# Graph layers on one core: weighted neighbour rows in fixed places with TensorE's source pass as a loop, and edge feature dots as GpSimd products summed by VectorE

## The reference, cut to what matters

```python
# layer 0: attention over the edges that end in a node
h = x @ Wn.T + bn
e = edge_attr @ We.T + be
a = leaky_relu(sum((h[src] + e) * attn, -1), 0.01)
a = softmax of a over the edges with the same dst
x = layernorm(x + relu(segment_sum(h[src] * a, dst)))
# layer 1: mean over neighbours (the roles turn: grouped by src, neighbour is dst)
mean = segment_sum(x[dst], src) / max(count(src), 1)
x = layernorm(x + x @ W1.T + b1 + mean @ W2.T + b2)
```

## Time and profile before

| | |
|---|---|
| median of the runs | 1409.51 us |
| the profiled execution's own time | 1417.53 us |
| its span, first to last instruction | 1415.7 us |
| TensorE busy | 1199.2 us, 85% of the span |
| VectorE busy | 1014.9 us, 72% |
| ScalarE busy | 705.8 us, 50% |
| GpSimd busy | 750.6 us, 53% |
| mean granted TensorE clock | 0.924 |

### The profile page before, as it was taken

How to read it: one execution, slowest core, us unless ns; L and a number is a source line. 1 busy time by engine, 2 the same in 40 slices (tenths; PEclk the granted TensorE clock), 3 DMA queues, 4 the chain that set the end, 5 groups by cost and what they waited for, 6 DMA issues and landing times.

```text
span 1415.7 us, 24884 instructions
## 1 busy us (share of the span) xinstructions
PE 1199.2 (85%) x6829; PEld 1043.3 (74%) x6829; DVE 1014.9 (72%) x3558; ACT 705.8 (50%) x1643; POOL 750.6 (53%) x731
## 2 busy tenths in 40 slices
PE   5988968990099999949999999999988888888884
PEld 5977847880078888838888888888877777777773
DVE  8377897888455555349999999999986656565551
ACT  4655564550034444427777766667763343434332
POOL 1047772767767777744444106656532555556533
PEclk9989999995589999979999999999998888988887
DMA  7779885979436666557777778999962332223211
GB/s 232 256 156 218 198 251 160 280 214 362 148 65 93 101 95 93 71 132 247 244 238 243 250 242 297 311 329 323 326 226 60 90 89 92 86 92 92 90 50 40
DMA packets 118168, 254.24 MB, mean 180 GB/s; under 512 B 23705, under 2 KB 63272, under 8 KB 118084
## 3 DMA queue, kind: packets, MB, share of 16 engines
q1 hardware_dynamic: 75738, 187.26, 41.6%
q0 software_dynamic: 40128, 64.45, 20.1%
q10 hardware_dynamic: 2218, 1.53, 0.3%
HBM read 175.67 MB, written 130.44 MB: 216 GB/s over the span
## 4 chain that ended last, share of the span: by engine, by line
PE 71%; DVE 9%; issue 8%; DMA 5%; ACT 4%; POOL 2%; SPq 1%; ACTq 0%; DVEq 0%; POOLq 0%
PE bank L1378 41%; PE bank L1367 8%; PE bank L1355 5%; PE bank L1427 3%; PE bank L1431 3%; PE bank L1521 3%; PE bank L1277 3%; DVE stats L957 3%; DVE X L784 2%; DMA X<-in_x,idx_src 2%; ACT aggn L631 2%; ACT sel L685 1%; PE bank L1314 1%; DVE xin L784 1%; POOL X L482 1%
## 5 line engine op out<-in xcount | busy, mean ns | idle before, releaser
L1378 PE MATMUL bank<-w1T,xT 128*128 128x256 f32 x1968 | 481.3, 392 | 1.8 <-ACT yout L594 1.8
L1378 PEld LDWEIGHTS bank<-w1T,xT 128*128 128x128 f32 x1968 | 379.1, 197 | 55.9 <-ACT xT L584 2.2
L492 POOL DMA_INDIRECT order_scratch<-pay,rank_i x200 | 195.8, 979 | 218.4 <-DVE xin L784 90.3
L589 ACT ACTIVATE std<-stats,eps_c 128x4 f32<-128x4 f32 x271 | 80.5, 298 | 278.0 <-DVE stats L957 278.0
L584 ACT ACTIVATE xT<-bank 128x512 f32<-128x512 f32 x296 | 176.8, 598 | 82.7 <-PE bank L1367 78.1
L594 ACT ACTIVATE yout<-bank,rstd 128x256 f32<-128x256 f32 x492 | 203.9, 480 | 0.7 <-DVE rstd L1023 0.5
L532 POOL DMA_INDIRECT z_scratch<-xin,idx_out x100 | 156.3, 1563 | 53.9 <-ACT xin L711 30.7
L957 DVE BATCH_NORM_STATS2 stats<-bank 128x6 f32<-128x512 f32 x246 | 167.8, 691 | 10.3 <-PE bank L1378 10.2
L957 DVE BATCH_NORM_STATS2 stats<-xin 128x6 f32<-128x512 f32 x240 | 154.6, 685 | 22.1 <-DMA xin<-z_scratch 22.1
L1378 PE MATMUL bank<-w2T,xT 128*128 128x256 f32 x400 | 126.8, 447 | 50.5 <-issue 49.8
L1355 PE MATMUL bank<-sel,agg 128*128 128x196 f32 x800 | 156.2, 339 | 0.0
(11 more groups left out here) (248 smaller groups left out, 1729.3 us busy)
## 6 DMA issues: line engine op xcount, KB each, us to landing
z_scratch<-in_x SPq DMA_DIRECT2D x125, 400.0 KB
xin<-z_scratch SPq DMA_DIRECT2D x97, 512.0 KB
out_rows<-yout SPq DMA_DIRECT2D x97, 512.0 KB, 3.2
kB<-sorted_scratch SPq DMA_DIRECT2D x50, 256.0 KB, 3.5
yout<-low_digits_scratch SPq DMA_DIRECT2D x50, 128.0 KB, 6.6
yout<-keys_scratch SPq DMA_DIRECT2D x50, 128.0 KB, 5.7
yout<-in_edge_attr SPq DMA_DIRECT2D x12, 512.0 KB, 5.8
order_scratch<-pay,rank_i POOLq DMA_INDIRECT x200
```

What stands on the lines that cost most here:

```text
L492: g.indirect_dma_start(out=order_dram[k], out_offset=bass.IndirectOffsetOnAxis(ap=rank_i[k][:, t:t + 1], axis=0), in_=pay[:, t, :], in_off ...
L1378: ins = mm(to, buf[:, jj, c, 0:n], w[:, c, :], start=not bias and i == 0 and c == 0, stop=i == len(terms) - 1 and c == 1)
```

## The change

It has two parts that do not touch each other.

**Edge feature dots.** `u` is made as 128 equal rows (`u_b`) by a product with 128 columns where there was one. GpSimd multiplies each loaded chunk by it in place (14 `tensor_tensor`, twelve of 128x1024 and two of 128x128), and VectorE sums each row of 128 into `pay` (14 `tensor_reduce`). Seven of the sums stand among the one-hots, after every second group from the 13th on; seven come behind the bias work. TensorE loses 98 turns and 196 small products, ScalarE 25 copies, and VectorE 25 high one-hots, which go to ScalarE (two a group where there was one; on the source side it stays one). SyncE reloads a buffer when its sum is done.

**Source pass.** ScalarE multiplies the four neighbour tiles of a turn by their factors and writes them to tiles 0 to 3 or 4 to 7 of X. The four `sel` tiles become one comparison without a factor. TensorE now reads fixed places, so its turns 4 to 23 become a loop, four turns a round.

```diff
+BY_ACT = (2, 1)
-            for c in range(4, NEC + FT + 1 - NEC * EC):
-                sp.wait_ge(s_eaT, 2 * (c - 3))
+            for c in range(4, NCH):
+                sp.wait_ge(s_eau, c - 3)
                 load_edges(c)
                 copy_x(2)
-            sp.wait_ge(s_eaT, Q)
+            sp.wait_ge(s_eau, NCH)
...
-            pool.wait_ge(s_eau, 1)
+            pool.wait_ge(s_wcp, 4)
+            for c in range(NCH):
+                pool.wait_ge(s_ea[c % 4], 16 * (c // 4 + 1))
+                part = chunk_rows(c)
+                n, k = part.shape[0], part.shape[1]
+                g.tensor_tensor(part, part, u_b[0:n, :].unsqueeze(1).to_broadcast([n, k, DE]), ALU.mult).then_inc(s_eap, 1)
+
+            pool.wait_ge(s_eau, NCH)
...
             def high_onehots(k, q):
-                n = k * Q + q
-                wait(act, s_hotA, n - 3)
-                t = GT * q + GT - 1
-                o = gap_hi[n % 4]
-                made = gap(o, iota16[:, 0:HC], -1.0, dig_f[k][:, 1, t:t + 1])
-                is_zero(onehot_hi[:, t, :], o, made).then_inc(s_hotA, 1)
+                for i in range(BY_ACT[k]):
+                    t = GT * q + GT - BY_ACT[k] + i
+                    n = hots_before(k, q) + i
+                    wait(act, s_hotA, n - 3)
+                    o = gap_hi[n % 4]
+                    made = gap(o, iota16[:, 0:HC], -1.0, dig_f[k][:, 1, t:t + 1])
+                    is_zero(onehot_hi[:, t, :], o, made).then_inc(s_hotA, 1)
...
+            def weigh_neighbours(q, u):
+                act.wait_ge(s_nw, q + 1)
+                wait(act, s_agg[SRC], 2 * (q - 1))
+                for j in range(GT):
+                    rows = X[:, bass.ds(q * GT + j, 1), 0:D].rearrange("p a c -> p (a c)")
+                    a.activation(X[:, u % 2 * GT + j, 0:D], rows, ACT.Copy,
+                                 scale=rstd[:, 4 + u % 2, j:j + 1]).then_inc(s_stage, 1)
+
+            weigh_neighbours(0, 0)
...
+                if in_range(q, 0, Q - 1):
+                    weigh_neighbours(q + 1, u + 1)
                 if in_range(q, 0, Q - 2):
                     root_neighbours(q + 2, u)
...
+            def edge_dots(c):
+                t = chunk_tile(c)
+                part = chunk_rows(c)
+                n, k = part.shape[0], part.shape[1]
+                if c == NCH - 1:
+                    then(v.memset(pay[:, FT:T, 2], 0.0))
+                dve.wait_ge(s_eap, c + 1)
+                v.tensor_reduce(pay[0:n, t:t + k, 2], part, X_AXIS, ALU.add).then_inc(s_eau, 1)
...
-                    if t % GT < GT - 1:
+                    if t % GT < GT - BY_ACT[k]:
                         ts(onehot_hi[:, t, :], iota16[:, 0:HC], dig_f[k][:, 1, t:t + 1], None, ALU.is_equal)
                     if t % GT == GT - 1:
                         ins.then_inc(s_onehot, 1)
+                        if k == DST and t % (2 * GT) == GT - 1 and t >= 12 * GT:
+                            edge_dots((t - 12 * GT) // (2 * GT))
...
-                dve.wait_ge(s_rc[slot], 2 * turn + 2)
-                for j in range(GT):
-                    ins = ts(sel[par][:, j, :], kB[par][:, j, :], keyc[SRC][:, bass.ds(q * GT + j, 1)],
-                             rstd[:, slot, j:j + 1], ALU.is_equal, ALU.mult)
-                ins.then_inc(s_sel[SRC], 1)
+                v.tensor_tensor(sel[par][:], kB[par][:], keyc[SRC][:, now].unsqueeze(2).to_broadcast([P, GT, P]),
+                                ALU.is_equal).then_inc(s_sel[SRC], 1)
...
-            edge_dots()
+            for c in range((Q - 12 + 1) // 2, NCH):
+                edge_dots(c)
             starts(DST)
...
+                        pe.wait_ge(s_stage, GT * q + 2 * p + 2)
                         for jj in range(2):
                             for c in range(2):
-                                rows = X[:, bass.ds(q * GT + 2 * p + jj, 1), c * P:(c + 1) * P].rearrange("p a c -> p (a c)")
+                                rows = X[:, u % 2 * GT + 2 * p + jj, c * P:(c + 1) * P]
...
-            for q in range(Q + 1):
-                by_src(q, q // 4, q % 4)
+            steps(pe, Q + 1, 4, 4, 2, by_src)
```

More of the change, by code:

```diff
@@ L73, in build @@
     NEC = FT // EC
+    NCH = NEC + FT + 1 - NEC * EC
     NCOPY, CR = 125, 5
@@ L301, in build @@
         s_carry = sem("carry_added")
+        s_nw = sem("neighbour_weights")
+        s_stage = sem("neighbours_weighted")
         def wait_apart(eng, sem, value):
@@ L316, in grp, with chunk_tile, chunk_rows @@
                 .rearrange("p a f -> p (a f)")
+        def chunk_tile(c):
+            return c * EC if c < NEC else NEC * EC + c - NEC
+        def chunk_rows(c):
+            t = chunk_tile(c)
+            return edge_rows[c % 4][0:P if t < FT else LT, 0:EC if c < NEC else 1, :]
         def spread(dram, q):
@@ L622, in _ @@
             a.copy(v_b[:], bank[3][:, 0:D])
-            a.copy(u_c[:], bank[4][:, 0:1])
+            a.copy(u_b[:], bank[4][:, 0:DE])
             a.copy(c0[:], bank[5][:, 0:1]).then_inc(s_wcp, 1)
@@ L821, in _ @@
             v.tensor_tensor(bsum[:], bsum_c[:, 0, :], bsum_c[:, 1, :], ALU.add).then_inc(s_attnb, 1)
-            def edge_dots():
-                then(v.memset(pay[:, FT:T, 2], 0.0))
-                dve.wait_ge(s_ead, Q)
-                v.tensor_copy(pay[:, 0:FT, 2], bank[0][:, 0:FT])
-                v.tensor_copy(pay[0:LT, FT:FT + 1, 2], bank[0][0:LT, FT:FT + 1]).then_inc(s_eau, 1)
+            def edge_dots(c):
+                t = chunk_tile(c)
+                part = chunk_rows(c)
[4 more added lines that the diff above has]
+                v.tensor_reduce(pay[0:n, t:t + k, 2], part, X_AXIS, ALU.add).then_inc(s_eau, 1)
             def onehots(k):
@@ L1044, in select_src @@
                 v.reciprocal(rstd[:, slot, :], std[:, slot, :]).then_inc(s_rc[slot], 1)
-                dve.wait_ge(s_rc[slot], 2 * turn + 1)
-                v.tensor_tensor(rstd[:, slot, :], rstd[:, slot, :], weight[:, now], ALU.mult).then_inc(s_rc[slot], 1)
+                dve.wait_ge(s_rc[slot], turn + 1)
+                v.tensor_tensor(rstd[:, slot, :], rstd[:, slot, :], weight[:, now], ALU.mult).then_inc(s_nw, 1)
                 dve.wait_ge(s_kb3[SRC][par], 16 * (turn + 1))
@@ L1266, in _ @@
             for b in range(2):
-                mm(bank[4][:, 0:1], weT[:, b, :], attn_c[:, b:b + 1], start=b == 0, stop=b == 1)
+                mm(bank[4][:, 0:DE], attn_b[:, b, :], weT[:, b, :], start=b == 0, stop=b == 1)
             for b in range(2):
@@ L1292, in shift_ordered @@
                 mm(o[:, 3 * P:3 * P + T], lastrow[:], keyc[k][:, 0:T], start=True, stop=True).then_inc(s_next, 1)
-            def edge_tiles(g):
-                return range(GT * g, min(GT * g + GT, FT + 1))
-            def edge_rows_of(t):
-                return P if t < FT else LT
-            def turn_edges(g):
-                for t in edge_tiles(g):
-                    c, i = (t // EC, t % EC) if t < NEC * EC else (NEC + t - NEC * EC, 0)
-                    pe.wait_ge(s_ea[c % 4], 16 * (c // 4 + 1))
-                    n, j = edge_rows_of(t), t % GT
-                    if j == 0:
-                        wait(pe, s_eac, g - 1)
-                    ins = tr(bank[3 + g % 2][:, j * P:j * P + n], edge_rows[c % 4][0:n, i, :], ident[0:n, 0:n])
-                ins.then_inc(s_eaT, 1)
-            def dot_edges(g):
-                pe.wait_ge(s_eac, g + 1)
-                for t in edge_tiles(g):
-                    n, j = edge_rows_of(t), t % GT
-                    ins = mm(bank[0][0:n, t:t + 1], edge_turned[g % 2][:, j * P:j * P + n], u_c[:], start=True, stop=True)
-                ins.then_inc(s_ead, 1)
             def sort(k, after):
```

28 lines of the change are left out of this document (8 added, 20 removed).

## The result

| | before | after |
|---|---|---|
| median of the runs | 1409.47 us | 1425.69 us (1424.75 to 1426.54, 4 runs) |
| the profiled execution's own time (span) | 1417.53 (1415.7) | 1426.54 (1424.7) |
| TensorE, VectorE busy | 1199.2, 1014.9 us | 1170.1, 1035.4 us |
| ScalarE, GpSimd busy | 705.8, 750.6 us | 751.8, 783.7 us |

What follows compares the result with a forecast made beforehand. It took TensorE to bound the destination histogram, and TensorE's wait for ScalarE's copy plus the lowered clock to lengthen source-pass turns. Terms 13.9 + 1.2 + 2.0 = +17.1 on 1409.5 gave 1426.6 us, range 1403 to 1438.

Steps and rivals of the forecast that it cites:

- The hold: Destination histogram: each GpSimd product, taken as 2.0 us, stops VectorE's one-hots for its whole length.
- the walk: Destination histogram, step by step through one-hots, products, sums and reloads: scans start at 84.4 instead of 70.46.
- the row that I chose: Histogram: GpSimd's affine_select, 0.245 us for 128 columns, used to price a product of 1024 columns at 2.0 us.
- From the scans to the end: After the histogram: the later start of the scans, +13.9 us, was added in full to the kernel's time.
- the 13.9: Histogram term: scans of the destination histogram start 13.9 us later.
- Start +1.2: Start of the source pass: ScalarE weighs turn 0 before its first root, +1.2 us, between 0.4 and 2.1.
- Loop +2.0: Source pass: TensorE's loop puts register arithmetic behind waits, 0.1 us a turn over 20 turns, +2.0 us.
- Rival 2: Source pass: a shifted gap keeps TensorE's clock up, 1.85 us back per spared turn, 1389.6 with all 20; chance 0.12.
- Rival 3: Source pass: ScalarE, with the weighing, becomes the bound of the turn, 9 us over 23 turns, 1436; chance 0.10.
- The source pass's +3.2: Source pass: cost of weighing turn 0 at its start, 1.2 us, and of TensorE's loop, 2.0 us.
- the main term: Destination histogram: GpSimd's products stop VectorE's one-hots, so the scans start 13.9 us later.
- 17.1: Whole kernel: forecast loss in us, from 13.9 in the histogram, 1.2 at the source pass's start and 2.0 for its loop.

Runs made afterwards that it cites:

- the idle products: Kernel before with a GpSimd memset and six 128x1024 GpSimd products whose result nobody uses, started when the weights are copied; 1408.41 us.
- the one-hots from PSUM: Changed kernel with VectorE's destination-side one-hots reading their row of numbers from PSUM (f32) instead of SBUF (bf16); 1428.52 us.
- the edges alone: Kernel before with only the histogram's part of the change (GpSimd products, VectorE sums, more high one-hots on ScalarE); 1422.61 us, ratio 1.0101.
- the first two runs with the copy moved: Changed kernel with ScalarE's copy of the first turned tiles ahead of the root, or still earlier, ahead of the y rows; 1350.68 and 1349.62 us.
- the run with `scalar_tensor_tensor`: Changed kernel with VectorE's one-hots made by scalar_tensor_tensor (equal, then plus a zero row) in place of tensor_scalar, GpSimd products kept; 1488.69 us.
- the source pass alone: Kernel before with only the source pass's part of the change (ScalarE weighs neighbour rows, one-shape selections, TensorE loop); 1407.3 us, ratio 0.9987.
- the copy first on before: Kernel before with ScalarE's copy of the first turned tiles ahead of the root, and nothing else; 1344.25 us, ratio 0.9528.

## Why the prediction was right

**The hold: right.** The step "a product holds VectorE's one-hots for its whole length" stood on one cast of 2.83 us; the idle products and the one-hots from PSUM have now shown it. Its sizes: a product takes 2.37 us, not 2.0; a sum 1.20, not 1.3. The end of the walk was another than the chain's: the walk ended over the reload of the last full chunk and gave the two single tiles 1.0 us, while the chain goes over the reload of the last single tile, issued behind the tenth sum and two copies of `x` (78.82 to 80.06), which the walk left out. Scans at 86.44 where 84.4 were forecast, +16.0 instead of +13.9. This execution is a late one, with its first one-hot at 12.70: the edges alone and the first two runs with the copy moved have the same histogram, their one-hots begin at 11.5, and their scans start at 83.59, 83.87 and 82.95. The estimate of 2.25 us a product, from the Trainium skill's "GPSIMD Engine Reference", section 3.1, was nearer than the row that I chose.

The Trainium skill's page "SBUF — State Buffer", section "Who interferes with whom", has rules that bear on this. By it `tensor_reduce` never contends. The runs agree: 1.21 us beside a product. By it a VectorE instruction with at most one SBUF input, in no two-port mode, doesn't contend with GpSimd either. The runs agree: 0.35 us beside products, from PSUM. By it one with two SBUF inputs contends with a GpSimd instruction that reads SBUF, and the order of issue decides who waits. The run with `scalar_tensor_tensor` agrees that either engine can wait, but its product, ready at 20.34, stood while some fifty one-hots were still to begin, and no run here tests the order.

**From the scans to the end: as forecast.** I added the 13.9 in full. Of the 16.0 only 12.1 reach the dense pass, which looks as if something were given back, but single executions spread as far. Four profiles have the older histogram (before, the source pass alone, the idle products, the copy first on before): scans at 70.0 to 71.0, last gather landed 308.4, 302.2, 304.2 and 303.0 us later. Four have the new one (the changed kernel, the edges alone, the first two runs with the copy moved): scans at 83.0 to 86.4, last gather landed 305.9, 303.3, 303.4 and 302.0 us later. By the medians of four, the scans come 13.1 us later, the last gather 13.0 and the source pass's first products 13.2: the term was right, and it is kept to the end.

**Start +1.2: wrong.** From the dense pass's last load on the chain to the first products it is 47.3 us before and 47.1 after; nothing was paid.

**Loop +2.0: wrong.** 13.72 us a turn against 13.70: the loop costs some 0.02 us a turn, not 0.1. That its register work hides in a gap in which TensorE waits anyway is likely, but not shown.

**Rival 2, in part.** Three turns with a short first piece (1075.63, 1101.11, 1113.05) where before had one (1063.78): two turns of 1.7 us, 3.4 us, which is more than the 2.8 by which the pass is shorter. The forecast had no term for it, and since the older source pass has spared turns in other runs, it is no effect of this change. The count and the stretch up to the last gather (308.4 us, 4 to 6 more than in the three other profiles) may also be why the profiled execution of before lies above its median: it has 23 long pieces, and the run with idle products, 1408.41 us, has 20. A second profile of before, which would settle it, was not taken.

**Rival 3: out at this length of turn.** The four weighings take 1.69 us, not 2.08, and ScalarE still idles 1.05 us or more before the root that follows the y rows.

So the mechanism of the main term was right, and that 17.1 came out within a microsecond of 16.2 is in part luck. The source pass's +3.2 was not paid: alone it is -0.8 us, with an interval that takes in zero. The histogram's 13.9 is 13.1 at the scans by the medians, and 14.5 us in time alone, with an interval of about 8 to 20 us. The 3 us between 13.1 and 16.2 are no more than what spared turns and the stretch before the last gather vary by from one execution to the next.

**What it passed over.** The prediction named the copy behind a root and the own statistics as what TensorE waits for, and priced the clock at 1.85 us a turn (5.38 less the second half's 3.53; against a spared first half, 3.69 to 3.72, it is 1.7), but treated the gap as given. That order was worth 67 us on the kernel before, four times the whole change.

## What to carry to other kernels

Before work is moved to GpSimd, look at what VectorE runs beside it: here bf16 one-hots with their row from SBUF (0.19 us) and a form with two operands from SBUF took turns with GpSimd, and VectorE doing the work itself was cheaper (1.2 against 2.4 us). Where an engine feeds TensorE, put the instruction whose input is ready ahead of the one that still waits: a gap cut from 2.1 to 1 us gave back the gap and the clock. And divide work so that no engine is the bound of the stage: with half of the dots on each of two engines the scans came at 64.97, with all on TensorE at 70.46 and with all on VectorE at 73.53 (the first of these runs also moved the bias work, so the division is not its only difference).

## What was not expected of the hardware

- GpSimd does not always win: with one-hots of 0.38 us issued back to back, a product ready at 20.34 ended only at 42.9, about one product's length after VectorE ran dry.
- A held VectorE instruction is filed as busy: 9.45 us with five one-hots read as full use. Counts in windows show it, shares do not.
- After gaps of 2.0 to 2.3 us the granted clock fell in most turns, not in all, and in varying number (16 to 23 of 23 turns). The length of the gap does not tell which: the spared turns of the changed kernel follow gaps of 2.01 and 2.06 us. After gaps of about 1 us or less (once 1.5), in the three runs that only move the copy, no long piece stands on the chain.
